# Layer 0 of a graph kernel, edge by edge: gathered rows of x times W1, float32r one-hot stacks, and W2 applied to sums per target node

## The chip, the core and the metric

The kernel runs on one core of a Trainium2 chip. The metric is the device time in microseconds (us) of one execution; the kernel before takes 5028.3 us, the median of three runs (5008.02 to 5033.12). The engines named below are TensorE (PE, with its weight loads as PEld), VectorE (DVE), ScalarE (ACT), GpSimd (POOL) and SyncE (SP), which only issues DMAs here. Each engine works through its own program in order and waits on semaphores.

## The reference

There are 12500 nodes with 48 features (x) and 200000 edges (src, dst), sorted by dst. Two layers follow each other, each with a residual and a layer norm:

```
layer 0:  h   = relu(concat(x[dst], x[src], e32) @ W1 + b1)      # 200000 x 128, W1 is 128 x 128
          msg = h @ W2 + b2                                      # W2 is 128 x 48
          x1  = layernorm(x + segment_sum(msg, dst))
layer 1:  m   = relu(x1[src] + e48)
          out = layernorm(x1 + (1 + eps) * x1 + segment_sum(m, dst))
```

The layer norm is over the 48 features, with no scale or offset. All arrays are float32.

## The kernel before

The edges are worked in 391 groups of 512 (4 tiles of 128 edges); 4 groups make an iteration of the loop. Since the edges are sorted by dst, the targets of one group lie within a window of 48 consecutive nodes. A prologue finds the window starts (base_row) and, for every edge, its place in the window (rel). If a group were wider than a window, a general path would be taken by a branch; with these inputs the windowed path runs.

Layer 0, for group u, as the engines do it:

- POOL gathers x[src] with four indirect DMAs, one for each tile, 128 rows of 48 floats each, into columns 48 to 96 of the tile edge (L427). It waits for S0["trans"] of four groups back, since there are four buffers.
- SP loads the 32 edge features into columns 96 to 128 of edge (L325), the indices (L315) and the 48 columns of xT that belong to the window, x_win (L349). SP works in the order of loads0: at the start of an iteration it also waits for the rows of the iteration before (next_idx).
- DVE writes the one-hot of the place in the window into columns 0 to 48 of edge, four instructions (L828).
- PE turns the four tiles by transposes into ps_t (L653), multiplies the window's rows by the first 48 rows of W1 (ps_a, L655), and ACT copies both to SBUF (edgeT, L526; w_edge, L534). One float32 matmul of 512 columns gives the hidden layer with features on partitions (ps_h, L662); ACT adds b1 and applies relu (hT, L538).
- One group later PE applies W2 to each tile (ps_m, L639), DVE adds b2 (msg, L848), PE sums the messages into the window by the one-hot (ps_sums, L629), and DVE adds the 48 x 48 result to the node sums acc (L844).

The order on each engine is written out by hand in one function for each engine (steps0). In the last 18 full iterations the layer norm of finished chunks of 1250 nodes is woven in (to_nodes L709, squares L503, sum_squares L940, divide L947, split L960 and L962, zero_sums L860); there are 10 chunks, the last of them after the loop. A float32 matmul is two passes of PE, and the trace has a record for each pass.

Layer 1 gathers rows of x1, but PE takes over three of every sixteen tiles by float32r matmuls of 480 columns against all of x1 (pick_rows, L699); these are what PE mostly does in layer 1. The change leaves layer 1's own steps as they are and gives them other PSUM banks.

## Time and profile before

| | |
|---|---|
| median of 3 runs | 5028.3 us |
| the profiled execution | 5031.79 us |
| its span (first to last instruction) | 5030.0 us |
| mean granted TensorE clock | 0.74 of full speed |
| PE busy | 4067.2 us, 81% of the span |
| DVE busy | 1776.9 us, 35% |
| ACT busy | 795.1 us, 16% |
| POOL busy | 2686.4 us, 53% |
| DMA | 149.71 MB, mean 30 GB/s |

The profiled execution's own time is 1.8 us more than its span and within the range of the three runs. The busy shares are means over two layers that have different limits: layer 0 ends at 2690.86 us (the last addition to acc before the last chunk's norm), and layer 1 takes the rest. Waits and prices have to be read by layer.

### The profile page before, as it was taken

The numbers are of one execution on the slowest core, as the hardware profiler recorded it, in microseconds if no ns is written. First come the engines' busy times: TensorE is split into PE (matmuls) and PEld (weight loads), VectorE is DVE, ScalarE is ACT, GpSimd is POOL, SyncE is SP. The second block draws the span as 40 slices with busy tenths as digits, with TensorE's granted clock in tenths as the row PEclk, the third lists the DMA queues.
The fourth block names the chain that finished last, engine by engine and source line by source line (L and its number), as shares of the span: only waits on it lengthen the run. The fifth ranks groups of instructions, "written<-read, shape, count | busy, mean of one in ns | idle before, by whom it ended". The sixth has DMA issues, their size and how long they took to land.

```text
span 5030.0 us, 74330 instructions
## 1 busy us (share of the span) xinstructions
PE 4067.2 (81%) x19093; PEld 2851.7 (57%) x19093; DVE 1776.9 (35%) x4614; ACT 795.1 (16%) x1962; POOL 2686.4 (53%) x2838
## 2 busy tenths in 40 slices
PE   5778887787887787888888777887887787878998
PEld 3455454454554454455556666665666665656777
DVE  2111111111111111122224455554555555545665
ACT  1222222222222222222221000000000000000111
POOL 5555555555555555555554555555454555554554
PEclk7666666656556656566567888889888888888988
DMA  3111111111111111111111111111111111111111
GB/s 66 27 25 26 27 26 26 27 25 25 26 27 25 26 27 26 25 28 29 28 31 29 29 31 32 29 31 32 29 29 29 33 29 29 32 31 29 37 38 35
DMA packets 409363, 149.71 MB, mean 30 GB/s; under 512 B 335252, under 2 KB 408936, under 8 KB 409192
## 3 DMA queue, kind: packets, MB, share of 16 engines
q0 software_dynamic: 90688, 69.83, 9.4%
q1 hardware_dynamic: 316392, 75.92, 7.5%
q10 hardware_dynamic: 2258, 3.68, 0.4%
q8 instruction: 10, 0.16, 0.0%
q14 instruction: 15, 0.12, 0.0%
HBM read 144.37 MB, written 4.80 MB: 30 GB/s over the span
## 4 chain that ended last, share of the span: by engine, by line
PE 63%; issue 15%; another core or an unknown queue 15%; DVE 4%; DVEq 1%; ACT 1%; DMA 0%; ACTq 0%; SPq 0%
PE ps_h L699 16%; PE ps_h L662 10%; PE ps_m L639 8%; PE ps_sums L629 8%; PE ps_t L699 8%; PE ps_t L653 6%; PE ps_a L655 3%; PE ps_nodes L709 1%; DVE at_place L881 1%; PE ps_t L691 1%; DVE picked L889 1%; PE ps_m L691 1%; DVEq L840 1%; ACT w_edge L534 1%
## 5 line engine op out<-in xcount | busy, mean ns | idle before, releaser
L427 POOL DMA_INDIRECT edge<-x,idx x1564 | 1482.5, 948 | 1191.4 <-issue 518.8
L427 POOL DMA_INDIRECT edge<-x_dram,idx x1270 | 1203.7, 948 | 1126.5 <-issue 611.1
L699 PE MATMUL ps_h<-x_parts,at_place 125*128 125x480 f32 x3920 | 1056.1, 422 | 83.3 <-issue 82.0
L629 PEld LDWEIGHTS ps_sums<-edge,msg 128*48 128x48 f32 x6256 | 452.1, 155 | 1105.0 <-issue 1096.9
L629 PE MATMUL ps_sums<-edge,msg 128*48 128x48 f32 x6256 | 567.7, 246 | 446.6 <-issue 274.6
L699 PEld LDWEIGHTS ps_h<-x_parts,at_place 125*128 125x128 f32 x3920 | 803.3, 211 | 220.9 <-issue 99.5
L662 PE MATMUL ps_h<-edgeT,w_edge 128*128 128x512 f32 x782 | 711.8, 1009 | 147.5 <-ACT w_edge L534 141.0
L844 DVE TENSOR_TENSOR acc<-acc,ps_sums 48x48 f32 x782 | 154.5, 198 | 1417.2 <-PE ps_sums L629 707.2
L699 PE MATMUL ps_t<-x_parts,at_place 125*128 125x480 f32 x1960 | 565.0, 425 | 100.7 <-issue 98.8
L639 PEld LDWEIGHTS ps_m<-w_sb,hT 128*128 128x128 f32 x3128 | 573.8, 275 | 127.3 <-issue 127.3
L639 PE MATMUL ps_m<-w_sb,hT 128*128 128x48 f32 x3128 | 630.5, 364 | 11.3 <-ACT hT L538 11.1
L848 DVE TENSOR_TENSOR msg<-ps_m,b_sb 128x192 f32<-128x192 f32 x391 | 139.7, 357 | 1158.6 <-remote 668.1
L699 PEld LDWEIGHTS ps_t<-x_parts,at_place 125*128 125x128 f32 x1960 | 406.7, 214 | 206.0 <-issue 150.0
L538 ACT ACTIVATE hT<-ps_h,b_sb 128x512 f32<-128x512 f32 x391 | 268.8, 687 | 1456.5 <-PE ps_h L662 670.5
L556 ACT ACTIVATE msg<-pre 128x192 f32<-128x192 f32 x391 | 141.7, 362 | 1842.3 <-DVE pre L909 915.8
L653 PE MATMUL ps_t<-ident_sb,edge 128*128 128x128 f32 x1564 | 388.6, 395 | 33.3 <-DMA x_win<-xT 23.4
L889 DVE SCALAR_TENSOR_TENSOR picked<-iota_sb,col_rest,ps_h 128x480 f32<-128x480 f32 x196 | 213.6, 1090 | 382.0 <-remote 183.7
L526 ACT ACTIVATE edgeT<-ps_t 128x512 f32<-128x512 f32 x391 | 233.1, 596 | 582.2 <-PE ps_t L653 268.9
L828 DVE TENSOR_SCALAR edge<-iota_sb,rel 128x48 f32<-128x48 f32 x1564 | 284.2, 254 | 60.3 <-issue 54.0
L653 PEld LDWEIGHTS ps_t<-ident_sb,edge 128*128 128x128 f32 x1564 | 252.2, 199 | 71.3 <-DMA x_win<-xT 23.5
L881 DVE TENSOR_TENSOR at_place<-ps_t,places_sb 125x1280 fp32r<-125x1280 f32 x197 | 291.7, 1481 | 0.0
L662 PEld LDWEIGHTS ps_h<-edgeT,w_edge 128*128 128x128 f32 x782 | 187.1, 294 | 159.5 <-ACT w_edge L534 153.0
(66 smaller groups left out, 1688.9 us busy)
## 6 DMA issues: line engine op xcount, KB each, us to landing
e_sb<-e SPq DMA_DIRECT2D x196, 192.0 KB
edge<-e SPq DMA_DIRECT2D x196, 128.0 KB
edge<-x,idx POOLq DMA_INDIRECT x1564
edge<-x_dram,idx POOLq DMA_INDIRECT x1270
idx<-src_tiles SPq DMA_DIRECT2D x392, 4.0 KB
x_win<-xT SPq DMA_DIRECT2D x391, 9.0 KB
acc<-xT ACTq DMA_DIRECT2D x1, 2343.8 KB, 24.4
x_dram<-feats SPq DMA_DIRECT2D x10, 234.4 KB
```

Source lines behind the costliest of these rows:

```text
L427: pool.indirect_dma_start(out=cols, out_offset=None, in_=rows_of, in_offset=bass.IndirectOffsetOnAxis(ap=index, axis=0)).then_inc(done, 16)
L526: nc.scalar.activation(edgeT[:, u % 2, :], ps_t[u % 2][:, :], ACT.Copy).then_inc(S0["edgeT"], 1)
L538: nc.scalar.activation(hT[:, u % 2, :], ps_h[u % 2][:, :], ACT.Relu, bias=b1_sb[:, :]).then_inc(S0["h"], 1)
L629: last = nc.tensor.matmul(sums, lhsT=msg[:, v % 2, t, :], rhs=edge[:, v, t, 0:WIN], start=(t == 0), stop=(t == TILES - 1))
L639: last = nc.tensor.matmul(ps_m[:, t, :], lhsT=hT[:, v % 2, t * P:(t + 1) * P], rhs=w2_sb[:, :], start=True, stop=True)
L653: last = nc.tensor.transpose(ps_t[u % 2][:, t * P:(t + 1) * P], edge[:, u, t, :], ident_sb[:, :])
L662: nc.tensor.matmul(ps_h[u % 2][:, :], lhsT=w_edge[:, u, :], rhs=edgeT[:, u % 2, :], start=True, stop=True).then_inc(S0["pre"], 1)
L699: last = nc.tensor.matmul(ps_picked[m], lhsT=at_place[:, m, c, :], rhs=x1_parts[:, c, part, :], start=(c == 0 and part == 0), stop=(c == C ...
L828: last = nc.vector.tensor_scalar(edge[:, (u + ahead) % UNROLL, t, 0:WIN], iota_sb[:, :], rel[:, bass.ds(i * UNROLL + u + ahead, 1), t], No ...
L844: nc.vector.tensor_tensor(acc[0:D, bass.ds(first, WIN)], acc[0:D, bass.ds(first, WIN)], ps_s[(u - back) % 2 if S is S1 else 0], ALU.add).t ...
L881: nc.vector.tensor_tensor(at_place[:, m, :, :], ps_place[m % 2].unsqueeze(1).to_broadcast([NP, CHUNKS, P]), places_sb[:, :].unsqueeze(2).t ...
L889: nc.vector.scalar_tensor_tensor(picked[:, :, :].rearrange("p f k -> p k f"), iota_sb[:, 0:CB].unsqueeze(2).to_broadcast([P, CB, D]), col_ ...
```

## The change

Layer 0 is built up anew; layer 1 and the general path keep their arithmetic.

- **A table.** Ahead of the loop PE multiplies all of x by the middle 48 rows of W1 (w1_src): 100 matmuls of 125 nodes by 128 features. ACT copies them out of PSUM (30 copies) and SP stores ten chunks of 640 KB to b_dram. Only then may the gathers of layer 0 start, and they fetch rows of 128 floats of this table, straight into the layout edge by feature. xT now comes in ten pieces on SP's queue.
- **Stacks.** A tile's stationary operand is now a stack (float32r, features on partitions, edges as columns): 48 rows of a one-hot of the window, computed directly in this layout by comparing dst ids, which SP loads broadcast to 48 partitions, twice (load_ids), and the edge features as a high and a low float32r part, turned by two transposes a group. Two tiles share a pair of 64-partition halves.
- **The moving operand** is w_edge, 256 columns: high and low parts of the window's product with W1 (with b1 as a 49th row) and of the edge features' weights. Four float32r matmuls a group write ps_h, edges on partitions; DVE adds both halves to the gathered rows (mix).
- **Relu and sums.** ACT and DVE write relu(h) as high and low parts beside a column of ones (h_parts); PE sums it over the edges into 48 x 258 by a one-hot (float32r). ACT copies the sums, PE turns them (turn_sums), and only then applies W2, once for 48 nodes instead of to 512 edges; b2 is added times the number of edges.
- The work is spread over slots with a lead of 1 or 2 groups (edge features) and lags of 1 to 4 groups (sums, turn, output, acc). The norm steps of two half chunks move to the second of two iterations.

```
-        x_win = sb("x_win", [D, UNROLL, WIN])
-        w_edge = sb("w_edge", [P, UNROLL, H])
-        edgeT = sb("edgeT", [P, 2, GE])
-        hT = sb("hT", [H, 2, GE])
+        x_win = sb("x_win", [SIDE, UNROLL, 2, SIDE])
+        w_edge = sb("w_edge", [P, 2, 2, 2 * H], F32R)
+        e_parts = sb("e_parts", [P, 2, TILES, 2 * DE], F32R)
+        sums_sb = sb("sums_sb", [WIN, 2, HS])
+        sumsT = sb("sumsT", [H, 2, WIN])
...
+            def load_ids(done, i, slot):
+                for p in (0, SIDE):
+                    sp.dma_start(dst_row[p:p + WIN, slot:slot + 2, :].rearrange("p g e -> p (g e)"),
+                                 dst_groups[bass.ds(i, 1), slot * GE:(slot + 2) * GE].to_broadcast([WIN, 2 * GE])).then_inc(done, 16)
...
-                        gather(edge[:, u, t, D:2 * D], rows_of, idx[:, u, t:t + 1], S["rows"][u])
+                        gather(edge[:, u, t, :] if S is S0 else edge[:, u, t, D:2 * D], rows_of, idx[:, u, t:t + 1], S["rows"][u])
...
-                others(S0, x, "trans")
+                wait_b_dram(pool)
+                gathers(S0, b_dram, "split", 0)
+                others(S0, b_dram, "split")
...
+            for n, c, first, end in thirds():
+                if first == 0:
+                    pe.wait_ge(s_xT[c], 16)
+                if n >= 4:
+                    pe.wait_ge(s_b_rows, n - 3)
+                for k in range(first, end):
+                    node = c * CN + k
+                    last = nc.tensor.matmul(ps_b[n % 4][0:NP, (k - first) * H:(k - first + 1) * H],
+                                            lhsT=acc[0:D, node:node + (NP - 1) * CB + 1:CB], rhs=w1_src[:, :], start=True, stop=True)
+                last.then_inc(s_b_nodes, 1)
...
+            def hidden(i, u):
+                b = u % 2
+                wait_group(pe, S0["mix"], i, u, back=1)
+                wait_group(pe, S0["alo"], i, u)
+                wait_group(pe, S0["spread"], i, u)
+                wait_group(pe, S0["edgeT"], i, u)
+                for t in range(TILES):
+                    j, side = divmod(t, 2)
+                    rows = P if side else SIDE + WIN
+                    last = nc.tensor.matmul(ps_h[:, t, :, :].rearrange("p a h -> p (a h)"), lhsT=stack[0:rows, b, j, side, :],
+                                            rhs=w_edge[0:rows, b, side, :], start=True, stop=True)
+                last.then_inc(S0["pre"], 1)
...
+            def sum_hidden(i, u, back):
+                for t in range(TILES):
+                    last = nc.tensor.matmul(ps_seg, lhsT=onehot_sb[:, b, t, :], rhs=h_parts[:, b, t, :],
+                                            start=(t == 0), stop=(t == TILES - 1))
...
+            def spread_ids(i, u, back):
+                for side in range(2):
+                    first = SIDE * (1 - side)
+                    ids = dst_row[first:first + WIN, v % UNROLL, :].rearrange("q (e j s) -> q s j e", j=2, s=2)
+                    last = nc.vector.tensor_scalar(stack[first:first + WIN, v % 2, :, side, :], ids[:, side, :, :],
+                                                   win_row[first:first + WIN, bass.ds(i * UNROLL + v, 1)], None, ALU.is_equal)
...
+            def mix(i, u):
+                wait_group(dve, S0["pre"], i, u)
+                dve.wait_ge(S0["rows"][u], i * (16 * TILES) + 16 * TILES)
+                nc.vector.tensor_tensor(edge[:, u, :, :], edge[:, u, :, :], ps_h[:, :, 0, :], ALU.add).then_inc(S0["first"], 1)
+                wait_group(dve, S0["first"], i, u)
+                nc.vector.tensor_tensor(edge[:, u, :, :], edge[:, u, :, :], ps_h[:, :, 1, :], ALU.add).then_inc(S0["mix"], 1)
...
+            def relu_low(i, u):
+                nc.vector.scalar_tensor_tensor(h_parts[:, b, :, H:2 * H], edge[:, u, :, :], 0.0, h_parts[:, b, :, 0:H].bitcast(F32),
+                                               ALU.max, ALU.subtract).then_inc(S0["split"], 1)
```

PE's program before, one group inside the loop of layer 0 (ps_t are the turned tiles, ps_m the messages):

```order
L653 MATMUL ps_t<-ident_sb,edge 128x128 [waits s0_rows1,s0_edgeT,s0_onehot]
L653 MATMUL ps_t<-ident_sb,edge 128x128 x3
L655 MATMUL ps_a<-w_dst,x_win 48x128
L639 MATMUL ps_m<-w_sb,hT 128x48 [waits s0_h,s0_msg]
L639 MATMUL ps_m<-w_sb,hT 128x48 x3
L662 MATMUL ps_h<-edgeT,w_edge 128x512 [waits s0_edgeT,s0_h,s0_stat]
L629 MATMUL ps_sums<-edge,msg 48x48 [waits s0_msg,s0_acc]
L629 MATMUL ps_sums<-edge,msg 48x48 x3
```

PE's program in the changed kernel at the same place (shared holds the stacks, the one-hots and h_parts; ps_eT the turned edge features):

```order
L798 MATMUL ps_h<-w_edge,shared 128x256 [waits s0_edgeT,s0_spread,s0_alo]
L798 MATMUL ps_h<-w_edge,shared 128x256 x3
L807 MATMUL ps_eT<-ident_sb,e_parts 128x128 [waits s0_elo]
L807 MATMUL ps_eT<-ident_sb,e_parts 128x128
L815 MATMUL ps_a<-w_dst,x_win 112x128 [waits s0_window1]
L825 MATMUL ps_hsum<-shared 48x258 [waits s0_split,s0_onehot,s0_sums]
L825 MATMUL ps_hsum<-shared 48x258 x3
L834 MATMUL ps_turned<-ident_sb,sums_sb 128x48 [waits s0_sums,s0_turned]
L834 MATMUL ps_turned<-ident_sb,sums_sb 128x48
L843 MATMUL ps_sums<-sumsT,w_sb 48x48 [waits s0_turned,s0_degree,s0_acc]
L844 MATMUL ps_sums<-ident_sb,b_deg 48x48
```

The hidden layer now stands first in a slot and works on group u; the transposes and the window's product belong to group u+1, the sums to u-1, the turn to u-2 and the output to u-3. The eight W2 matmul passes and the 512-column matmul are gone.

DVE's program before, one group inside the loop:

```order
L828 TENSOR_SCALAR edge<-iota_sb,rel 128x48 [waits s0_seg]
L828 TENSOR_SCALAR edge<-iota_sb,rel 128x48 x3
L848 TENSOR_TENSOR msg<-ps_m,b_sb 128x192 [waits s0_msgp,s0_seg]
L840 TENSOR_LOAD base_row
L840 ISA x2
L844 ISA [waits s0_seg,s0_acc]
L844 TENSOR_TENSOR acc<-acc,ps_sums 48x48
```

DVE's program in the changed kernel, one group inside the loop:

```order
L1063 TENSOR_TENSOR e_parts<-e_sb,e_parts 128x4x32 [waits s0_ehi]
...
L1074 TENSOR_SCALAR shared<-resid_sb,win_row 48x2x128
...
L1074 TENSOR_SCALAR shared<-resid_sb,win_row 48x2x128
L1082 TENSOR_TENSOR edge<-edge,ps_h 128x512 [waits s0_rows1,s0_pre]
L1084 TENSOR_TENSOR edge<-edge,ps_h 128x512 [waits s0_first]
...
L1091 TENSOR_SCALAR b_deg<-b_sb,sums_sb 48x48 [waits s0_sums,s0_out]
...
L1037 TENSOR_TENSOR acc<-acc,ps_sums 48x48
...
L1095 TENSOR_TENSOR shared<-iota_sb,rel 128x192
L1104 TENSOR_TENSOR w_edge<-ps_a,w_edge 48x128 [waits s0_ahi]
L1104 TENSOR_TENSOR w_edge<-ps_a,w_edge 48x128
L1111 SCALAR_TENSOR_TENSOR shared<-edge,shared 128x4x128 [waits s0_h]
```

DVE now has eleven arithmetic instructions a group where it had six, among them three over 512 columns. It, and no longer PE, waits for the gathered rows.

## Rows read from the trace of the kernel before

**Rows 1.** Busy time by stretch: start:end, length, each engine's us, PEclk, DMA share, GB/s.
```profile
10.00:20.00 10.00, 2.24 (x4) 1.01 (x4) 8.20 (x15) 1.49 (x2) 7.87 (x8) 1.00 1.33 214
...
500.00:1000.00 500.00, 400.90 (x1793) 250.10 (x1792) 93.92 (x449) 111.73 (x225) 280.60 (x297) 0.63 0.18 26
3500.00:4000.00 500.00, 393.78 (x1970) 303.07 (x1970) 257.54 (x441) 36.41 (x147) 255.04 (x269) 0.87 0.15 30
```

**Rows 2.** Instructions in order, one group of layer 0: start, us, engine, line [idle before].
```profile
1002.79 0.85 PE L629 MATMUL ps_sums<-edge,msg 128*48 128x48 f32 x8 [3.32 <-issue]
...
1003.76 1.11 PE L653 MATMUL ps_t<-ident_sb,edge 128*128 128x128 f32 x4
...
1004.80 0.66 PE L655 MATMUL ps_a<-w_dst,x_win 48*48 48x128 f32 x2
...
1005.39 1.94 PE L639 MATMUL ps_m<-w_sb,hT 128*128 128x48 f32 x8
...
1007.46 0.95 POOL L427 DMA_INDIRECT edge<-x,idx  x1 [2.71 <-remote]
...
1007.48 2.07 PE L662 MATMUL ps_h<-edgeT,w_edge 128*128 128x512 f32 x2
...
1008.71 0.95 POOL L427 DMA_INDIRECT edge<-x,idx  x1 [0.30 <-issue]
1009.48 0.15 PEld L629 LDWEIGHTS ps_sums<-edge,msg 128*48 128x48 f32 x1 [1.50 <-issue]
```

**Rows 3.** Groups of instructions, 500 to 1500 us: busy us, mean ns, idle before.
```profile
L427 POOL DMA_INDIRECT edge<-x,idx x589 | 557.4, 946 | 441.9 <-issue 190.9 <-PE ps_t L653 143.2 <-DMA idx<-src_tiles 71.3
```

**Rows 4.** PE's instructions in order, two stretches of layer 1.
```profile
3501.26 3.75 PE L699 MATMUL ps_h<-x_parts,at_place 125*128 125x480 f32 x16
...
3522.77 4.75 PE L699 MATMUL ps_t<-x_parts,at_place 125*128 125x480 f32 x11
```

**Rows 5.** Groups of DVE's and ACT's instructions over the whole span, shapes kept apart.
```profile
L889 DVE SCALAR_TENSOR_TENSOR picked<-iota_sb,col_rest,ps_h 128x480 f32<-128x480 f32 x196 | 213.6, 1090 | 382.0 <-remote 183.7 <-PE ps_h L699 125.9 <-PE ps_t L699 41.4
...
L844 DVE TENSOR_TENSOR acc<-acc,ps_sums 48x48 f32 x782 | 154.5, 198 | 1417.2 <-PE ps_sums L629 707.2 <-remote 548.1 <-issue 157.3
...
L909 DVE TENSOR_TENSOR pre<-edge,e_sb 128x192 f32<-128x192 f32 x391 | 136.4, 349 | 6.1 <-issue 5.7
...
L935 DVE SCALAR_TENSOR_TENSOR resid_sb<-feats,res_scale,ps_nodes 125x240 f32 x18 | 8.4, 464 | 53.5 <-remote 33.6 <-PE ps_nodes L709 17.2 <-issue 2.7
...
L526 ACT ACTIVATE edgeT<-ps_t 128x512 f32<-128x512 f32 x391 | 233.1, 596 | 582.2 <-PE ps_t L653 268.9 <-remote 191.2 <-issue 121.9
...
L534 ACT ACTIVATE w_edge<-ps_a 48x128 f32<-48x128 f32 x391 | 103.5, 265 | 27.2 <-PE ps_a L655 12.8 <-remote 5.9 <-issue 0.2
```

**Rows 6.** Gathers on POOL beside DVE's instructions, three places, in order of time.
```profile
17.27 0.51 DVE L819 TENSOR_SCALAR col_place<-resid_sb 128x392 f32<-128x392 uint32 x1
17.59 1.01 POOL L427 DMA_INDIRECT edge<-x,idx  x1 [0.30 <-issue]
...
18.82 0.85 DVE L822 TENSOR_TENSOR col_rest<-col_rest,resid_sb 128x392 f32<-128x392 f32 x1
18.91 1.59 POOL L427 DMA_INDIRECT edge<-x,idx  x1 [0.30 <-issue]
...
2452.57 0.95 POOL L427 DMA_INDIRECT edge<-x,idx  x1 [0.30 <-issue]
...
2453.42 0.41 DVE L962 TENSOR_TENSOR x_parts<-feats,x_parts  x1
```

**Rows 7.** First work of the loop, last sum of layer 0, and the last store of x1.
```profile
37.00 1.11 PE L653 MATMUL ps_t<-ident_sb,edge 128*128 128x128 f32 x4 [23.38 <-DMA x_win<-xT]
...
2690.86 0.20 DVE L844 TENSOR_TENSOR acc<-acc,ps_sums 48x48 f32 x1 [0.88 <-PE ps_sums L629]
...
2697.68 0.31 SPq L309 DMA_DIRECT2D x_dram<-feats  x1
...
2702.30 0.95 POOL L427 DMA_INDIRECT edge<-x_dram,idx  x1 [28.00 <-DMA x_dram<-feats]
```

More of the change, by code:

```diff
@@ L203, in build @@
         s_iota = sem("s_iota")
-        N_CONST = 16
+        N_CONST = 17
         def layer_sems(n):
-            per_slot = {"idx": 2, "edges": 2, "window": UNROLL, "rows": UNROLL}
-            counts = ("onehot", "awin", "stat", "trans", "edgeT", "pre", "h", "msgp", "sum", "msg", "seg", "acc",
-                      "parts", "zeroed", "column", "row", "places", "ten", "picked", "staged", "nodes",
-                      "resid", "square", "var", "std", "rstd", "norm")
+            per_slot = {"idx": 2, "edges": 2, "rows": UNROLL}
+            counts = ("onehot", "seg", "acc", "staged", "nodes", "square", "var", "std", "rstd", "norm")
+            if n == 0:
+                per_slot = {**per_slot, "window": UNROLL, "ids": 2}
+                counts += ("ehi", "elo", "trans", "edgeT", "spread", "awin", "ahi", "alo", "pre", "first", "mix", "h",
+                           "split", "sums", "degree", "turn", "turned", "out", "parts", "zeroed", "resid")
+            else:
+                counts += ("sum", "msg", "resid", "column", "row", "places", "ten", "picked")
             return {**{w: sems(f"s{n}_{w}", k) for w, k in per_slot.items()}, **{w: sem(f"s{n}_{w}") for w in counts}}
@@ L478, in general @@
             def general():
-                for u in range(UNROLL):
-                    pool.wait_ge(S0["rows"][u], 16 * TILES)
                 general_layer(G0, 0)
@@ new lines, in window_high, with relu_high @@
+            def window_high(i, u, back):
+                b = (u - back) % 2
+                wait_group(act, S0["pre"], i, u, back=back + 2)
+                wait_group(act, S0["awin"], i, u, back=back)
+                for side in range(2):
+                    first = SIDE * (1 - side)
+                    last = nc.scalar.activation(w_edge[first:first + WIN, b, side, 0:H], ps_a[first:first + WIN, :], ACT.Copy)
+                last.then_inc(S0["ahi"], 1)
+            def relu_high(i, u):
+                b = u % 2
+                wait_group(act, S0["seg"], i, u, back=2)
+                wait_group(act, S0["mix"], i, u)
+                nc.scalar.activation(h_parts[:, b, :, 0:H], edge[:, u, :, :], ACT.Relu).then_inc(S0["h"], 1)
@@ new lines, in copy_sums, with copy_turned @@
+            def copy_sums(i, u, back):
+                b = (u - back) % 2
+                wait_group(act, S0["turn"], i, u, back=back + 2)
+                wait_group(act, S0["degree"], i, u, back=back + 2)
+                wait_group(act, S0["seg"], i, u, back=back)
+                nc.scalar.activation(sums_sb[:, b, :], ps_seg, ACT.Copy).then_inc(S0["sums"], 1)
+            def copy_turned(i, u, back):
+                b = (u - back) % 2
+                wait_group(act, S0["out"], i, u, back=back + 2)
+                wait_group(act, S0["turn"], i, u, back=back)
+                nc.scalar.activation(sumsT[:, b, :], ps_sumsT, ACT.Copy).then_inc(S0["turned"], 1)
@@ new lines, in steps0 @@
+            def steps0(i, c):
+                for u in slots0(i):
+                    if exists(i, u, 0):
+                        hidden(i, u)
+                    if exists(i, u, -1):
+                        transpose_edges(i, u, -1)
+                        window_rows(i, u, -1)
+                    if exists(i, u, 1):
+                        sum_hidden(i, u, 1)
+                    if exists(i, u, 2):
+                        turn_sums(i, u, 2)
+                    if exists(i, u, 3):
+                        output_layer(i, u, 3)
+                    if c is not None and c[1] == 1 and u == 0:
```

415 lines of the change are left out of this document (283 added, 132 removed).

## The prediction

> **What bounds the kernel now.** I read the busy time by stretch first, since the page's shares are means over two layers. In [rows 1], layer 0 (500 to 1000 us) has PE busy 401 of 500 us at a granted clock of 0.63 and POOL busy 281; layer 1 (3500 to 4000 us) has PE at 394 us and 0.87. The clock has two levels, 1.2 and 2.4 GHz, so layer 0 runs mostly at the lower. Next the instructions in order, for one group of layer 0 [rows 2]: PE's five pieces take 0.85 + 1.11 + 0.66 + 1.94 + 2.07 = 6.63 us, and the next group's first piece begins at 1009.48, 6.69 us after 1002.79. So PE alone sets the pace at the lower clock; ACT's and DVE's pieces lie beside it. POOL's gathers follow each other at 1.25 us (1007.46 to 1008.71, 0.95 busy and 0.30 issue): four need 5.0 us and then wait [rows 2, 3]. Layer 0 ends at 2690.86 [rows 7], after 391 groups from about 37 us, or 6.79 us each. What remains to the end, 5030.0 - 2690.9 = 2339 us, is layer 1 and the last norm; 1.8 us lie outside the span.
>
> **PE's part.** Prices by the column, at the lower clock, since that one is the harder:
> - hidden, 4 float32r matmuls of 256 columns. Eleven of 480 columns took 4.75 us in a slow stretch, 0.90 ns a column, and sixteen took 3.75 us in a fast one, 0.49 [rows 4]. So 4 x 0.23 = 0.92 us (0.50 fast). The other bound is float32: 2.07 us for 512 columns [rows 2], or 4.1 us for the four. I take 0.92, as the rows have this very type.
> - two transposes, half of 1.11: 0.56. The window's product, two passes as before: 0.66.
> - sum_hidden, 4 of 258 columns: 0.93.
> - turn_sums, 4 passes of 128 x 48, half of L639's eight: 0.97. Output, 4 passes of 48 x 48, half of L629's: 0.43.
>
> Sum 4.47 us against 6.63. The eight W2 passes (1.94) and the 512-column matmul (2.07) go. PE falls below POOL's 5.0, even at 1.2 GHz, so no gain from the clock is counted.
>
> **DVE's part.** From 198 ns at 48 and 349 ns at 192 columns [rows 5]: 1.05 ns a column and 0.15 us each; L935 (464 ns for 240) adds 0.06 for a per-partition scalar. So edges_low (128) 0.28; spread_ids 2 x 256 columns 0.96; mix 2 x 512 columns 1.37; degrees 0.26; accumulate 0.20; onehot 0.35; window_low 2 x 128 columns 0.56; relu_low (512) 0.69. Sum 4.67 us, where DVE had 93.92 us in 500 [rows 1], 1.3 a group. The two spreads may run at two columns a cycle (about 4.4 in all). The high bound is the costliest instruction of the trace, L889, 1090 ns for 480 columns, 2.27 ns a column [rows 5]; with it for spread, mix and relu DVE needs 0.28 + 1.16 + 2.32 + 0.26 + 0.20 + 0.35 + 0.56 + 1.16 = 6.3. L889 writes every tenth word and the new ones write in order, like L935 and L909, so I take 4.67.
>
> **ACT's part.** 265 ns at 128, 596 ns at 512 [rows 5]: 0.86 ns a column. Turned edges 2 x 0.38, window 2 x 0.27, relu 0.60, sums (258) 0.38, turned 0.20, edges_high 0.27: 2.7 us, hidden.
>
> **The chain across engines.** hidden(u+1) waits for mix(u) and for window_low(u+1) on DVE, which waits for ACT's two copies, which wait for transposes and window product, which stand behind hidden(u) on PE: 0.92 + 0.56 + 0.66 + 0.54 + 0.56 and a few waits, about 3.5 us. The other half, mix 1.37 and then DVE's rest, is DVE's own 4.67. Neither reaches 5.0. SP loads the window of an iteration's first group only behind next_idx, that is, once the last group's rows are in; a store and its landing took 4.6 us here [rows 7], and a window a few. With POOL as the bound these rows arrive late and PE waits there, once in four groups; the four buffers let POOL go on meanwhile, so I add nothing and keep it for the range.
>
> **POOL is the new bound.** Same four gathers, 5.0 us a group, if a gather of 512-byte rows costs POOL what one of 192 bytes does. The trace has no other row length; POOL's 0.95 us are for 128 rows either way, and I take no change. DMA engines: a group moves 262 KB of rows, 197 KB of ids, 64 KB of features and some 20 KB more, 540 KB in 5.3 us or 102 GB/s, against 214 GB/s reached at 10 to 20 us [rows 1]. Covered, though it makes landings later.
>
> **POOL held by DVE.** In [rows 6] a gather that starts at 18.91 in the middle of L822, which has two SBUF inputs and ends at 19.67, takes 1.59 instead of 0.95 us: it gains 0.64, the 0.76 that were left less 0.12. One that starts in L819 with 0.19 left gains 0.06. The one at 2452.57, in progress when L962 (two SBUF inputs) starts, gains nothing. So a gather pays only where it starts inside such an instruction. The new slot has edges_low, onehot and relu_low of that kind, and perhaps the spreads. For a gather at a random moment the gain is the sum of (d - 0.12)^2 over twice the period: (0.03 + 0.05 + 0.32 + 0.26)/10.6 = 0.06 us, 0.25 for four. Bounds 0 and, with each instruction met at its start, 1.7. I take 0.3, so 5.3 us a group.
>
> The Trainium skill (SBUF — State Buffer, "SBUF: two separate sides") calls the shared port pair an exclusive lock, held for the whole instruction, in which the other side fully blocks, and warns that a VectorE instruction in a two-port mode keeps GpSimd from writing descriptors. [...]
>
> **The prologue.** The table is 100 matmuls of two passes over 128 columns. By L653's 0.28 us a pass [rows 2] this is 56 us at 1.2 GHz, about 30 if fast; ACT's 30 copies of at most 0.6 hide in it. xT arrives in pieces. The last of ten stores follows: 640 KB each. At 214 GB/s one takes 3.0 us and hides behind PE's 5.6 a chunk; by x1's last store (4.6 us from issue to the next gather for 234 KB [rows 7]) it would be 12.6. Start 8 + 56 + a store of about 9 gives the first gather at 73, I take 75; bounds 45 (fast PE) and 140 (stores in series). Before, the loop began at 37.
>
> **The sum.** 75 + 391 x 5.3 (2072) + 10 for the last rows to land and the lagging stages to empty + 15 for the woven-in norm steps (eleven instructions a chunk of about L962's 0.41 us [rows 6], 4.5 us of DVE for each of nine chunks, 40 in all; the slack of 0.6 us in each of 8 groups, 4.8 a chunk, would hide it if it were spread evenly, and I take a third as lost) = 2172, against 2691. Then 2339 as before, whose steps stay, and 1.8: **4513 us**. The profiled execution (5031.8) stands 3.5 above the median, within its runs, so I leave it at that and say 4513.
>
> **Rivals.**
> 1. *The slot doesn't close at POOL's rate.* DVE's 4.67 plus waits at each handover (mix after hidden, window_low after ACT, relu_low after relu_high), and late windows, give 5.9 us. For: DVE is 88% full and crosses to PE and ACT three times a slot. Against: PE before kept 6.69 with 6.63 of work. Time: 4513 + 0.6 x 391 = 4748.
> 2. *Clean gathers,* phases such that none starts inside a two-input instruction, and a faster prologue: 5.0 us and 50: 4370.
> 3. *Slower: DVE at L889's price.* 6.3 us of work and 0.5 of waits, 6.8 a group: 75 + 2659 + 25 + 2341 = 5100. It decides from 6.64 us a group on, where 391 groups eat the whole saving. Against it speak L909 and L935.
> 4. *Slower: the port is held at any overlap.* Then a gather waits for all of 0.28 + 0.35 + 0.69 + 0.96 us in turn, 7.3 a group: 5290. The row at 2452.57 speaks against it [rows 6]. [...]
> 5. *Gathers cost by the byte.* 0.95 x 512/192 = 2.5 us, 11.3 a group: 6860. Only the number of rows, 128 in all gathers, is seen to be constant, so it isn't excluded.
>
> **How the numbers follow.** Forecast 0.62 (its own range 4400 to 4640, from 5.0 to 5.6 us a group), rival 1 0.24, rival 2 0.06, rival 3 0.03, rival 4 0.02, rival 5 0.02, and 0.01 for no effect that can be told. The range for 8 in 10 is 4390 to 4780: 5.0 to 5.95 us a group. A measurement of this kernel can tell about 0.5% from no change (the runs of before lie within 0.5%). Faster: 0.62 + 0.24 + 0.06 = 0.92; same 0.01; slower 0.07.
>
> **What would show it.** Right: POOL's gathers follow at 1.25 us with few gaps from about 75 to 2150 us and DVE's first mix instruction waits for the rows; a group at 5.3; layer 1 as long as before; gathers of 1.2 to 1.6 us that start inside L1063, L1095 or L1111; PE near 4.5 us a group at the low clock. Rival 1: POOL waits for S0["split"] (L1111), and DVE has no idle time or has it behind PE or ACT. Rival 3: L1082 or L1111 over 1.0 us. Rival 4: gathers longer wherever DVE reads two inputs. Rival 5: gathers over 1 us with DVE idle. It would be wrong at its root if float32r at 256 columns cost like float32, or if layer 1 lost time by its new banks.

## The result, and the profile after

The changed kernel takes 5288.3 us, the median of four runs (5259.19 to 5299.72), beside 5025.5 for the kernel before (5008.02 to 5033.12): a ratio of 1.052, 95% interval 1.047 to 1.057. It is 5.2% slower; the forecast was 4513 us. A second comparison in another job gave 5214.7 against 4925.0, 1.060 (1.056 to 1.064).

One plain fact must be told first, since no number below can be read without it. The kernel before itself took 4910 to 5033 us in some jobs and 3686 to 3737 us in others, close together within each job. It isn't the chip: the one with number 2 took 4910 to 4944 us in one job and 3691 to 3704 us in another half an hour later. I call these *held* and *free* jobs, for what the traces will show. The forecast, the two results above and the profiles of before and after are from held jobs. Every experiment is read against the kernel before in its own job.

Where the difference lies. Layer 0 ends where layer 1's first gather starts; in the profile after, three rows tell the stages (minimum, median and longest duration in ns, then first and last start):

```profile
L515 POOL DMA_INDIRECT edge<-b_dram,idx x1564: 941/947/1822, 79.3 to 2911.5; - x196
```
```profile
L1082 DVE TENSOR_TENSOR edge<-edge,ps_h x391: 662/686/690, 86.0 to 2926.5; 128x512 f32<-128x512 f32 x196
```
```profile
L515 POOL DMA_INDIRECT edge<-x_dram,idx x1270: 941/947/1179, 2946.7 to 5258.7; - x182
```

The loop starts at 79 instead of 37, 42 us later. Layer 1 starts at 2946.7 instead of 2702.3 [rows 7]. From there to the end it is 2338.5 us, against 5030.0 - 2702.3 = 2327.7 before, 11 us more. (In the second job it was 28 us less, 2277 against 2305, so that is no cost of the change.) So 244 of the 255 us are the prologue and layer 0.

The stages by windows (columns as in [rows 1], whose rows 500:1000 and 3500:4000 these two answer):

```profile
500.00:1000.00 500.00, 348.33 (x1385) 257.24 (x1384) 294.43 (x756) 168.00 (x548) 266.54 (x278) 1.00 0.32 75
3500.00:4000.00 500.00, 431.39 (x1985) 310.25 (x1984) 254.18 (x434) 35.60 (x144) 256.47 (x271) 0.71 0.16 30
```

From 500 to 1500 us 138 groups pass (L1082 has 138 instructions there), 7.25 us each; before, 297 gathers in 500 us are 74 groups, 6.74 us each. No engine is busy over 70% of layer 0, POOL 53%. The page's slices say the same over the whole run, layer 0 up to slice 22:

```profile
PE   5667766666767766767777888888888888888998
DVE  2566555555655655556666554555455455545666
POOL 2555555555555555555555454555545555555554
PEclk9999999999999999999999877667777677777777
```

**PE's clock in layer 0.** The 1.00 and the 9s must not be read as full speed. The trace of after has no clock record before 2950 us, while that of before begins at 47 us, and a stretch without a record prints as 1.00. PE's own instructions tell the level. A transpose of 128 x 128 in the kernel before, in a stretch with a granted clock of 0.97, in one with 0.50 (windows 992:999 and 1003:1010), and at the very start, where 30:45 prints 1.00 though records begin only at 47; then the same kind of transpose after, over all of layer 0:

```profile
L653 PE MATMUL ps_t<-ident_sb,edge x8: 272/273/335, 992.4 to 996.9; 128*128 128x128 f32 x8
L653 PE MATMUL ps_t<-ident_sb,edge x8: 421/421/476, 1003.8 to 1011.0; 128*128 128x128 f32 x8
L653 PE MATMUL ps_t<-ident_sb,edge x8: 417/421/472, 37.0 to 41.6; 128*128 128x128 f32 x8
```
```profile
L807 PE MATMUL ps_eT<-ident_sb,e_parts x782: 415/421/478, 79.8 to 2921.5; 128*128 128x128 f32 x196
```

So PE ran the whole of the changed layer 0 at the lower level, 1.2 GHz. The same holds for every run below that is made from the changed kernel: none has a clock record ahead of layer 1, and none of their 782 such transposes took under 414 ns. Wherever their windows print 1.00 in layer 0, the lower level is meant. The windows of the kernel before at 500:1000 do have records.

What the engines wait for in 500 to 1500 us (engine, line, released by: total us, times, longest):

```profile
ACT shared L621 <- remote: 423.4, 58, 8.0
POOL edge L515 <- issue: 313.5, 521, 5.2
DVE edge L1082 <- remote: 271.0, 66, 5.9
POOL edge L515 <- DVE shared L1111: 153.3, 32, 6.1
```

"Remote" is a release that the profile finds no source for on this core. The program runs on one core, so it is no other core of its own. The kernel before has the same, in the same stretch:

```profile
DVE msg L848 <- remote: 257.2, 53, 8.1
...
ACT hT L538 <- remote: 235.4, 37, 8.4
```

One such wait in the timeline after (start, duration, instruction, idle time before it and what ended it):

```profile
995.20 0.31 ACT L657 ACTIVATE e_parts<-e_sb 128x128 fp32r<-128x128 f32 x1
...
995.57 1.22 PE L798 MATMUL ps_h<-w_edge,shared 112*128 112x256 f32 x4
...
996.59 0.63 PE L807 MATMUL ps_eT<-ident_sb,e_parts 128*128 128x128 f32 x2
...
997.10 0.95 POOL L515 DMA_INDIRECT edge<-b_dram,idx  x1 [0.30 <-issue]
...
998.35 0.95 POOL L515 DMA_INDIRECT edge<-b_dram,idx  x1 [0.30 <-issue]
...
1000.85 0.95 POOL L515 DMA_INDIRECT edge<-b_dram,idx  x1 [0.30 <-issue]
1001.33 0.69 DVE L1082 TENSOR_TENSOR edge<-edge,ps_h 128x512 f32<-128x512 f32 x1 [4.42 <-remote]
...
1003.33 0.39 PE L843 MATMUL ps_sums<-sumsT,w_sb 128*48 128x48 f32 x2 [3.38 <-issue]
...
1003.49 0.77 ACT L621 ACTIVATE shared<-ps_eT 64x256 fp32r<-64x256 f32 x2 [7.98 <-remote]
```

L621 needs nothing but the transposes L807, recorded as done at 997.2, and L798. It starts at 1003.5, and DVE's L1082, which needs L798 and the rows, at 1001.3, just as a run of eight gathers (991.94 to 1001.80) ends. After that POOL idles 5 us, as its next gathers wait for DVE, and the next pair of groups begins: a group of 5.7 to 6.4 us and one of 8.3 to 9.1 by turns, from L1082 to L1082 between 985.87 and 1015.32. The waits above say that it goes on so.

The trace's own semaphore records say which signal is late. The semaphore that L621 waits for is raised by PE behind the transposes; it is recorded at 1003.47, 6.3 us after their recorded end, and ACT starts 0.02 us later. In 63 of the 138 groups from 500 to 1500 us L621 starts more than 2 us after that end, and in 53 of the 63 within 0.1 us of such a record. In acc_wait_2, a free run (experiment 4), all 190 records stand within 0.02 us of the end. So in a held job PE's signal of being done comes late, or PE is done later than its modelled end says; what delays it is open.

It isn't the loading of instructions. The page's queue table has 11 and 18 packets on the two instruction queues in the whole run:

```profile
q8 instruction: 11, 0.18, 0.0%
q14 instruction: 18, 0.15, 0.0%
```

The Trainium skill (Runtime: NRT & Kernel Launch, "Instruction fetch mechanics") warns that a taken branch outside the two loaded pages of 16 KiB forces a fetch; the trace's packets have that size (0.18 MB / 11), but 29 of them can't be a fetch in each of 97 iterations. The counts are alike in held and free runs (10 and 15 in before, and in before_paced, a free one), and so is the time that the data packets take: 9.4% of 5030.0 us for the gathers' 90688 packets in before, 12.4% of 3748.0 in before_paced, 473 and 465 us.

### The profile page after: what moved, and what is told of

Its sections match the earlier page's. It is cut to its first block, busy times and chain, and to the rows that moved or that the text cites. A ratio compares the mean times of both kernels' runs of the same rounds, so it can differ in the third digit from the quotient of the medians.

```text
span 5285.2 us, 79584 instructions
## 1 busy us (share of the span) xinstructions
PE 4104.4 (78%) x17729; PEld 3039.9 (58%) x17729; DVE 2969.7 (56%) x6582; ACT 1195.8 (23%) x3948; POOL 2719.0 (51%) x2838
## 3 DMA queue, kind: packets, MB, share of 16 engines
q0 software_dynamic: 90688, 133.89, 12.3%
## 4 chain that ended last, share of the span: by engine, by line
PE 45%; another core or an unknown queue 25%; issue 14%; DVE 10%; ACT 3%; DVEq 2%; ACTq 1%; DMA 0%; SPq 0%
PE ps_h L894 17%; PE ps_eT L894 8%; PE ps_h L798 4%; PE ps_sums L784 3%; PE ps_hsum L825 3%; PE ps_turned L834 3%; DVE w_edge L1104 2%; PE ps_a L815 2%; ACT w_edge L631 2%; PE ps_eT L807 1%; DVEq L1032 1%; DVE shared L1074 1%; PE ps_nodes L904 1%; DVE edge L1082 1%
## 5 line engine op out<-in xcount | busy, mean ns | idle before, releaser
L515 POOL DMA_INDIRECT edge<-b_dram,idx x1564 | 1516.3, 969 | 1395.8 <-issue 855.9
L894 PE MATMUL ps_h<-x_parts,shared 125*128 125x480 f32 x3920 | 1167.0, 456 | 80.0 <-issue 78.5
L894 PEld LDWEIGHTS ps_h<-x_parts,shared 125*128 125x128 f32 x3920 | 812.6, 214 | 297.7 <-issue 95.5
L1082 DVE TENSOR_TENSOR edge<-edge,ps_h 128x512 f32<-128x512 f32 x391 | 265.7, 679 | 777.3 <-remote 700.9
L621 ACT ACTIVATE shared<-ps_eT 64x256 fp32r<-64x256 f32 x782 | 295.8, 378 | 1598.0 <-remote 1096.4
L798 PE MATMUL ps_h<-w_edge,shared 112*128 112x256 f32 (+1 forms) x1564 | 474.7, 455 | 233.1 <-DVE w_edge L1104 197.7
L894 PE MATMUL ps_eT<-x_parts,shared 125*128 125x480 f32 x1960 | 597.1, 453 | 48.6 <-issue 47.8
L798 PEld LDWEIGHTS ps_h<-w_edge,shared 112*128 112x128 f32 (+1 forms) x1564 | 362.4, 320 | 279.2 <-issue 151.1
L894 PEld LDWEIGHTS ps_eT<-x_parts,shared 125*128 125x128 f32 x1960 | 409.2, 214 | 178.2 <-issue 81.7
L834 PEld LDWEIGHTS ps_turned<-ident_sb,sums_sb 48*128 48x128 f32 x1564 | 362.0, 319 | 139.8 <-issue 139.7
L825 PE MATMUL ps_hsum<-shared 128*48 128x258 f32 x1564 | 427.7, 426 | 0.5 <-DVE shared L1111 0.5
L834 PE MATMUL ps_turned<-ident_sb,sums_sb 48*128 48x48 f32 x1564 | 424.9, 419 | 0.0
L807 PE MATMUL ps_eT<-ident_sb,e_parts 128*128 128x128 f32 x782 | 247.8, 421 | 85.7 <-DVE e_parts L1063 57.0
```

The lines of the kernel that those rows point to most:

```text
L515: pool.indirect_dma_start(out=cols, out_offset=None, in_=rows_of, in_offset=bass.IndirectOffsetOnAxis(ap=index, axis=0)).then_inc(done, 16)
L621: last = nc.scalar.activation(stack[side * SIDE:(side + 1) * SIDE, b, :, side, :], ps_eT[side * SIDE:(side + 1) * SIDE, 0, :, :], ACT.Copy)
L798: last = nc.tensor.matmul(ps_h[:, t, :, :].rearrange("p a h -> p (a h)"), lhsT=stack[0:rows, b, j, side, :], rhs=w_edge[0:rows, b, side, : ...
L807: last = nc.tensor.transpose(ps_eT[:, 0, j, :], e_parts[:, b, 2 * j:2 * j + 2, :].rearrange("p t f -> p (t f)").bitcast(F32), ident_sb[:, :])
L825: last = nc.tensor.matmul(ps_seg, lhsT=onehot_sb[:, b, t, :], rhs=h_parts[:, b, t, :], start=(t == 0), stop=(t == TILES - 1))
L834: last = nc.tensor.matmul(ps_sumsT, lhsT=sums_sb[:, b, a * H:(a + 1) * H], rhs=ident_sb[0:WIN, 0:WIN], start=(a == 0), stop=(a == 1))
```

## The experiments

Each edit is to the changed kernel unless said. "Left out after the first iteration" means that old data are used. Runs whose time is given without an interval were made once. Per group times are from the window 500:1000, where 20 PE instructions make a group of the changed kernel.

**1. The target ids.** Two broadcast loads of 192 KB come once in two groups, as the long waits do. DVE's wait for them goes with them.

```
-  wait_group(sp, S0["spread"], ...); load_ids(S0["ids"][u // 2], i, u)
+  if first_iteration(i): load_ids(S0["ids"][u // 2], i, u)
```

> The changed kernel with the broadcast loads of target ids (two of 192 KB per two groups) left out of layer 0 after the first iteration; stale ids are compared instead, the number of instructions on DVE stays. In the changed kernel a group of layer 0 takes 7.25 us, and on every second group DVE's first mix instruction (L1082) waits 4.4 us and ACT's turned edges (L621) 8 us, while POOL runs eight gathers in a row. Theory A, that the gathers running in a row are what holds the other engines: no change, 7.2 to 7.3 us a group, total 5240 to 5300. Theory B, that the bursts of ids clog the queue that everything else passes: the stalls go, 5.3 to 5.7 us a group, total 4520 to 4700.

**2. No gathers.** A semaphore is counted in their place, for layer 0 after the first iteration.

> The changed kernel with no gathers in layer 0 after the first iteration; POOL only counts, and DVE adds to old rows. Everything else stays. PE, DVE and ACT have 5.5, 4.8 and 3.1 us of work a group. Theory A: the stalls on L1082 and L621 vanish, and a group takes PE's 5.0 us or less, total about 4400 or below. Theory B (ids) or D (the wait of the output layer for the previous group's accumulate): the stalls of every second group stay, 6.5 us a group or more, total above 4950.

**3. Short rows.** Rows of x (192 bytes) instead of the table's 512; the rest of edge is set to zero at the start.

> The changed kernel gathering 48 floats (rows of x) instead of 128 in layer 0: as many gathers, 192 bytes a row instead of 512; the rest of each row in SBUF stays zero. Theory C, that the longer rows cause the stalls: 5.3 to 5.7 us a group, total 4520 to 4700. Theory A (it is the gathers being issued, not their bytes): 7.0 to 7.3 us a group, total 5190 to 5300.

**4. The accumulate's wait.**

```
 def output_layer(i, u, back):
-    wait_group(pe, S0["acc"], i, u, back=back + 1)
+    wait_group(pe, S0["acc"], i, u, back=back + 2)
```

On DVE the accumulate waits, instead, for DVE's own accumulate of the group before.

> The changed kernel with the output layer on PE waiting for the accumulate two groups back, as layer 1 does, instead of one (the accumulates are ordered on DVE itself). PE is idle 3.4 us before L843 in every second group. Theory D, that this wait closes a ring PE - DVE - PE: L843's idle time goes and a group takes 6 us or less, total 4800 or below. Theory A: PE runs on a little further and then waits in hidden (L798) instead, the group stays at 7.0 to 7.3, total 5190 to 5300.

This job was a free one: before took 3737 us. The four took 3882.6, 3792.5, 3879.8 and 3893.3 us, one run each. None of the four traces has a single remote wait, so each of my theories was asked in a place where the waits don't exist. What it showed is what the changed kernel is without them. Gathers of acc_wait_2, and the window of it and of no_gathers:

```profile
1003.62 0.95 POOL L515 DMA_INDIRECT edge<-b_dram,idx  x1 [0.30 <-issue]
1004.87 0.94 POOL L515 DMA_INDIRECT edge<-b_dram,idx  x1 [0.30 <-issue]
...
1016.61 1.46 POOL L515 DMA_INDIRECT edge<-b_dram,idx  x1 [0.30 <-issue]
```
```profile
500.00:1000.00 500.00, 474.17 (x1907) 353.62 (x1906) 420.59 (x1050) 245.86 (x764) 383.89 (x382) 1.00 0.41 104
```
```profile
500.00:1000.00 500.00, 500.00 (x2018) 374.24 (x2017) 442.75 (x1109) 258.89 (x807) 0.00 (x0) 1.00 0.23 57
```

The gathers follow without a pause: 382 in 500 us, one in 1.31 us, 5.24 us a group, with some stretched to 1.2 to 1.5. Bytes, ids and the accumulate's wait move nothing (3880 to 3893). Without gathers PE is busy all of the time and takes 500 / 100.9 = 4.96 us a group, at the lower clock.

**5. The same in a held job, and the kernel before beside it.**

> The kernel before, unchanged, for its profile beside the others. The same kernel took 5025 us beside the changed kernel and 3737 us beside the first four experiments, with PE at a granted clock of 0.86 instead of 0.73. Two explanations: the clock alone makes the difference (then every instruction of the profile is as before, PE's are shorter, and the waits of 4 to 8 us put down to an unknown source while POOL runs eight gathers stay); or the waits themselves are a property of how the program was running there and are gone (then none over 2 us is seen in layer 0, and POOL's 5.0 us a group or less is the pace, 1960 us for layer 0).

> The changed kernel, unchanged, timed against the kernel before on the same chip. If the program runs as in the first four experiments (before at about 3737 us), the changed kernel should stand at 3880 to 3900, 4% slower, since leaving out ids, row bytes or the wait for the accumulate moved nothing there; if it runs as at first (before at about 5025), 5259 to 5300. In the first case PE is the bound of layer 0 at 5.0 us a group at full clock.

For before_no_gathers the kernel before has its layer-0 gathers replaced by a count, as in 2.

> The kernel before with layer 0's gathers left out after the first iteration. Theory A (gathers in a row hold the others, and POOL's 5.0 us a group bounds the kernel before): layer 0 falls to PE's own work. At full clock that is 6.63 us at the lower level divided by at most 2, 3.4 to 4.5 us a group, 1370 to 1800 us for layer 0 instead of about 1960. Rival: PE is the bound of the kernel before in layer 0 on this chip also, and nothing moves.

> As no_gathers: the changed kernel without layer 0's gathers after the first iteration, beside the kernel before's own profile. If the program runs as in the first four experiments, 3790 us again: PE alone, 4.85 us a group. If it runs as at first (before at 5025), theory A says that the stalls of L1082 and L621 vanish and layer 0 takes 5.0 us a group or less, total 4400; the rival, an instruction supply that is slow whatever POOL does, keeps 6.5 us a group or more.

Measured: before 4935.0, after 5214.7, before_no_gathers 3815.6, no_gathers_again 4404.4. The windows of before_no_gathers and no_gathers_again:

```profile
500.00:1000.00 500.00, 490.49 (x3478) 319.35 (x3478) 180.49 (x868) 208.11 (x435) 0.00 (x0) 1.00 0.15 22
```
```profile
500.00:1000.00 500.00, 500.00 (x2018) 374.49 (x2018) 442.75 (x1109) 258.66 (x806) 0.00 (x0) 1.00 0.22 57
```

Without gathers the remote waits are gone from layer 0 of both (one of 1.0 us is left). The kernel before takes 3.45 us a group (435 ACT instructions, three a group) where it took 6.5, and 1119 us less in all; the changed kernel 4.96 where it took 7.0 (1421 PE instructions in after_again), and 810 us less. Layer 1, which kept its gathers, kept its waits. So in a held job taking the gathers away, and nothing of PE's work, frees both kernels. The two figures are at different clocks: without gathers the kernel before has PE at the upper level (its transposes take 273 ns in the median), the changed one keeps it at the lower (421), though PE is busy for all of the 500 us. At the lower level the change does cut PE's work, from 6.63 to 4.96 us a group.

**6. How many, in a row, or their traffic.** two_gathers leaves out two of four. paced adds one wait:

```
 wait_group(pool, S[read], i, u, back=UNROLL)
+if S is S0: wait_group(pool, S0["mix"], i, u, back=2)
```

plain_rows puts one plain load of 512 rows on SP in place of four gathers; pool_memset a memset of 1024 columns for each gather; before_paced holds the gathers of the kernel before until the transposes two groups back.

> The changed kernel with two of the four gathers of a group in layer 0, as two_gathers, which was run where before takes 3710 us and there gave 3791 (PE busy all the time, 4.96 us a group). Beside a kernel before of about 4925 to 5030: if every gather costs the others the same, 6.0 us a group and 4810; if only runs of more than four in a row do, 5.0 to 5.3 and 4410 to 4540.

> The changed kernel with its gathers also held until the mix of the group two back, as paced, which was 8.8% slower than before where before takes 3710 us. Beside a kernel before of about 4925 to 5030: if long runs of gathers hold the others, 5.3 to 6.2 us a group and 4530 to 4880; if each gather costs the same, 7.0 to 7.6 us and 5180 to 5400.

> The changed kernel with the four gathers of a group in layer 0 (after the first iteration) replaced by one plain load on SP of 512 rows of 512 bytes, the first of the table: the same bytes and the same number of rows in flight, but nothing that POOL writes. If the rows' traffic holds the others, the group stays above 6.5 us and the total above 4900 beside a kernel before of about 4925; if it is POOL's issue of gathers, 5.0 to 5.3 us a group, total 4410 to 4540. Where before takes 3710: 3790 to 3890.

> The changed kernel with each gather of layer 0 (after the first iteration) replaced by a POOL memset of 128x1024 float32 that no one reads: POOL is busy and counts as before, but nothing is written for a DMA and no rows move. If POOL being busy in SBUF (a port it shares) held the others, the waits of 4 to 8 us before L1082 and L621 stay in some measure, 6 us a group or more. If it is the gathers' own issue and DMAs, a group takes 5.0 us as with none (total 4400 beside a kernel before of 4925), or the memsets' own length if four are longer.

> The kernel before where POOL may start a group's gathers in layer 0 only when the group two back is transposed, instead of four back. Runs of eight gathers are cut to four. If long runs hold the others: layer 0 falls from 6.6 us a group towards POOL's 5.0, total 4300 to 4800 beside a kernel before of 4925. If each gather costs the same: 4900 to 4950.

Held job (before 4951.1 and, its own profile again, 4922.3): two gathers 4380.6, paced_2 5121.4, plain_rows 4410.3. Windows of two_gathers_2 and plain_rows:

```profile
500.00:1000.00 500.00, 500.00 (x2018) 374.47 (x2018) 444.48 (x1109) 258.51 (x806) 199.05 (x202) 1.00 0.34 83
```
```profile
500.00:1000.00 500.00, 500.00 (x2018) 374.40 (x2016) 442.91 (x1110) 258.58 (x806) 0.00 (x0) 1.00 0.42 111
```

Two gathers a group cost nothing, so it isn't a price for each gather. The same bytes in as many rows, at 111 GB/s in all, cost nothing, so it isn't the amount of traffic: what holds the others comes with POOL's gathers. (plain_rows reads the same 512 rows of the table each time and through SP's queue. So the scattered addresses and the gathers' own queue are left out with POOL's issue, and are not told apart from it.) The windows can't tell prices below PE's 4.96 us, which hides them. Pacing failed as a test of run length: in its trace runs of eight still occur (1009.44 to 1019.7), and up to 1020.9 to 1021.4 DVE's L1084 has stood idle for 4.3 us, ACT's L623 for 5.6 and PE's L817 for 4.4. Its 5121 us lie in neither expected range, 2% under the changed kernel of the second held job, which is too near to mean anything across jobs.

Free job (before 3709.5): two_gathers 3791.1, pool_memset 4228.6, paced 4039.8 (ratio 1.088, 1.081 to 1.095) and before_paced 3775.5 (1.019, 1.013 to 1.026; unclear by a bound of 2%). There pacing only delays: in paced SP's windows come late behind the rows that next_idx waits for (L817 waits 113 us in 1000 for x_win on PE, its weight load 131). pool_memset ran only here and so can't tell whether a busy POOL holds the others in a held job (experiment 7 bears on that); it shows another thing. Two DVE rows of it, and the same two instructions after:

```profile
L1090 DVE TENSOR_SCALAR shared<-resid_sb,win_row 48x256 fp32r<-48x256 int32 x327 | 369.2, 1129 | 7.7
...
L1101 DVE TENSOR_TENSOR edge<-edge,ps_h 128x512 f32<-128x512 f32 x164 | 112.5, 686 | 5.6
```
```profile
L1074 DVE TENSOR_SCALAR shared<-resid_sb,win_row 48x256 fp32r<-48x256 int32 x276 | 127.4, 462 | 6.5
L1084 DVE TENSOR_TENSOR edge<-edge,ps_h 128x512 f32<-128x512 f32 x138 | 94.8, 687 | 4.7
```

Beside POOL's memsets DVE's TENSOR_SCALAR takes 1129 ns instead of 462, and this TENSOR_TENSOR, with one input in SBUF and one in PSUM, is unchanged. So are those with both inputs in SBUF (L1079 276 ns for 282 after, L1112 370 for 359). The one exception is the accumulate of 48x48, 350 ns for 202, which isn't explained. Beside gathers neither of the two shown is longer: it is the gather that pays.

**7. At what rate.** Three gathers a group in layer 0, and in layer 1 a gap behind each gather:

```
 gather(...)
+if S is S1: nc.gpsimd.memset(busy_sb[:, :], 0.0)      # 128x512
```

> The changed kernel with three of the four gathers of a group in layer 0 (after the first iteration), and in layer 1 a POOL memset of 128x512 float32 that no one reads behind every gather. Beside a kernel before of about 4925 to 5030. Layer 0: three gathers take POOL 3.75 us of PE's 4.95 us a group. If the others are held whenever gathers come faster than one in about 1.8 us on average (7.2/4 here, 6.8/4 in the kernel before, 6.0/3.25 in layer 1), three give 5.4 us a group; if only POOL having no idle time holds them, 4.95 to 5.0; if each gather beyond two costs 1.1 us, 6.0. Layer 1: with the memsets a gather comes every 1.75 us at best, 5.7 us a group; if the gap relieves the others, layer 1 stays at 5.7 to 6.0 us a group (2230 to 2350 us); if the time that POOL spends is simply added, it rises to 6.5 or more. Where before takes 3710: layer 0 at 4.96 and layer 1 at 5.7 instead of 4.6.

Held job (before 5022.7): 4270.1 us, the fastest of all held runs. Its windows, and POOL in layer 1:

```profile
500.00:1000.00 500.00, 500.00 (x2017) 374.18 (x2017) 445.57 (x1108) 259.01 (x807) 308.64 (x304) 1.00 0.39 97
...
3000.00:3500.00 500.00, 417.22 (x2182) 333.39 (x2181) 294.11 (x482) 39.80 (x161) 445.59 (x598) 0.89 0.17 33
```
```profile
3504.88 0.95 POOL L520 DMA_INDIRECT edge<-x_dram,idx  x1 [0.17 <-POOL busy_sb L537]
3505.84 0.54 POOL L537 MEMSET busy_sb<- 128x512 f32 x1
3506.54 0.95 POOL L520 DMA_INDIRECT edge<-x_dram,idx  x1 [0.17 <-POOL busy_sb L537]
```

Three gathers in 4.96 us, one in 1.65 on average, cost nothing in this window either (a few remote waits, up to 7.3 us, stand elsewhere in layer 0). Within a group they still follow at 1.25 us, with a pause behind the third. And in layer 1, where POOL now has *more* to do and a gather follows in 1.66 us instead of 1.25, the remote waits are gone and the layer takes 4268.2 - 2123.7 = 2145 us instead of the 2266 to 2339 of the other held runs. That pace is POOL's own, 3.25 x 1.66 = 5.4 us a group, below both expected ranges; and POOL is busy there for 446 of 500 us, so a POOL that is busy with gathers and memsets in turn holds no one. So gathers hold the other engines, in a held job, when they go on at 1.25 us apart, and not when they come 1.66 us apart on average. Whether it is the mean rate, the pause, or POOL's wait between a gather and the next isn't told apart.

**8. The kernel before with gaps.**

> The kernel before, all of its work kept, with a POOL memset behind every gather: 128x256 float32 in layer 0, 128x384 in layer 1. By the 0.54 us of 512 columns and the 0.95 of 1024 these take about 0.33 and 0.43 us, and with the 0.95 of a gather and 0.17 between, a gather comes every 1.45 us in layer 0 (5.8 us a group) and every 1.55 in layer 1 (5.05). Beside a kernel before of about 4925 to 5030. If these gaps are enough: layer 0 falls from 6.7 to 5.8 us a group and layer 1 from 6.0 to 5.1, total 4150 to 4400, faster than both kernels by over 10%. If gathers must be 1.66 us or more apart: 4700 to 5000. If the time of POOL is simply added: 5100 and more. Where before takes 3710 us, no gathers hold anyone and POOL is the pace: 4200 to 4300, slower.

This job was a free one: 4338.1 us against 3699.4 (1.173, 1.170 to 1.175), slower as expected there (4200 to 4300). A gather came every 1.44 us in layer 0. Whether such a gap makes the kernel before faster in a held job wasn't run and stays open. No version beat both kernels with all of the work kept.

## Why the prediction was wrong, point by point

- **"So PE alone sets the pace at the lower clock": false, and the step that failed.** I took one group in which PE's instructions stood back to back [rows 2] for all of them, though its first row has 3.32 us of idle time before it. The window beside it said otherwise: 401 us busy in 500 over 74 groups is 5.4 us of PE a group, not 6.63 [rows 1]. A fifth of PE's time was idle, beside remote waits on DVE and ACT, and no term of the sum or rival stood for them. The change then cut PE's work at the lower clock from 6.63 to 4.96 us, and the group grew from 6.74 to 7.25: the saving was made on an engine that wasn't the pace. Without gathers the kernel before needs 3.45 us a group. For it the low clock was no fixed condition either: without gathers it read 1.00, by records, and its transposes took 273 ns. In the changed kernel the clock stayed low with gathers and without.
- **"PE falls below POOL's 5.0, even at 1.2 GHz": right, by a hair.** The sum was 4.47 us at the low clock and measured 4.96 there. Start to start in one group: hidden 1.02 for 0.92, transposes 0.56 for 0.56, window 0.69 for 0.66, sum 1.03 for 0.93, turn 1.01 for 0.97, output 0.65 for 0.43. My price by the column came from 480-column matmuls with a weight load each; here every 48 to 258 columns bring one, and those of the stacks are 0.23 us of busy time each (187.0 us for 808 in no_gathers_again). That this makes up the 0.49 us is likely, but no run shows it:

```profile
L805 PE MATMUL ps_h<-w_edge,shared 112*128 112x256 f32 (+1 forms) x808 | 246.4, 456 | 0.0
...
L805 PEld LDWEIGHTS ps_h<-w_edge,shared 112*128 112x128 f32 (+1 forms) x808 | 187.0, 320 | 18.3
```

  "So no gain from the clock is counted" came out true for the new kernel and missed what the old one could gain: 6.63 us at the lower level, 3.45 at the upper. What keeps PE at the lower level in the changed layer 0, even when it is busy without a break, wasn't tested.
- **"POOL is the new bound", 5.3 us a group: right in free jobs, wrong in held ones.** acc_wait_2 shows 5.24, from gathers stretched by DVE (1007 ns on average where 946 is the clean one), 0.24 us a group where I took 0.3. But POOL's 5.0 is nearly the pace of the kernel before there too: its paced form passes 397 gathers in 500 us. So nothing is won, and the prologue, the stretch and the norm's steps are lost: near 3890 against 3737. In held jobs the engines don't follow at 1.25 us, whichever kernel; 7.25 against 6.74 us a group. The term 391 x 5.3 was 1.95 us a group too small, 762 of the 775 us by which 4513 misses 5288.
- **"The buffers let POOL go on, so I add nothing": false in held jobs.** POOL goes on for eight gathers, then waits 5 us for DVE (L1111). Rival 1's sign, POOL waiting for the split, appeared, but with DVE 59% busy, not full: its mechanism was not this one.
- **DVE and ACT: right.** mix 2 x 0.69 (predicted 1.37 together), spread 0.91 to 0.97 (0.96), window_low 0.59 (0.56), relu_low 0.68 (0.69), relu 0.63 (0.60). Rivals 3 and 5 are out: nothing costs L889's price, and 512-byte rows cost POOL 947 ns as 192-byte ones did.
- **The port (rival 4): out.** A gather is 969 ns on average in layer 0, where rival 4 needed over half a microsecond more. By the Trainium skill (SBUF — State Buffer, "SBUF: two separate sides") the lock goes to whichever side starts first, and DVE takes it only in a two-port mode, or with two SBUF inputs against a GpSimd instruction that reads SBUF. The traces agree: the gather at 2452.57, begun before DVE's instruction, isn't stretched, and beside memsets TENSOR_TENSOR of 128x512 stays at 686 ns. The stretched TENSOR_SCALAR would fit a two-port mode, which no trace names; the accumulate's 350 ns for 202 doesn't fit.
- **The prologue and layer 1: right.** First gather at 79.3 for 75; layer 1 2338.5 for 2339. The norm and the drain cost more than the 25 us taken: in no_gathers_again layer 1 starts at 2106, where 79 + 391 x 4.96 is 2018.

The arithmetic of the loss in the first result: 391 x (7.25 - 6.74) = 199, the prologue 42, layer 1 11, in sum 252 of 255 us. Why a held group is half a microsecond longer after the change than before wasn't isolated. Between two waits the kernel before passes groups at the upper clock (4.1 us from transposes to transposes, 992.42 to 996.52), which the changed one can't at 4.96 us of PE; that would do it, and is only argued.

Open: what it is in a held job that the gathers take from the others. For layer 0 of the changed kernel it is shown, by single runs with effects of 800 us, that it goes away without POOL's gathers and with fewer of them, and that the same number of bytes and rows by SP's queue doesn't bring it on. Instruction loading is out by the packet counts. The ids and the length of the rows were varied only in a free job, where the waits don't exist, so a held job may still depend on them. In the profile after it is PE's signals that are recorded late; why is not shown.

## What to carry to other kernels

Divide an engine's busy time in a window by the groups in it before believing a tidy stretch of the timeline: 5.4 busy of 6.7 us is not a bound, and waits with no named source must be explained ahead of any saving. Check a printed clock against the duration of a known instruction: 1.00 here stood for missing records. Test what bounds a kernel by taking the suspected resource away (here the gathers: 1119 us) before rebuilding another engine's work. Time the unchanged kernel in more than one job.

## What the runs showed of the hardware

- The same program takes 3.69 to 3.74 or 4.91 to 5.03 ms in different jobs, on one chip even, and the difference appears with gathers 1.25 us apart.
- More work on POOL, a 0.54 us memset behind each gather, made layer 1 at least 5% shorter in a held job.
- A 128x128 transpose takes 273 ns at the upper clock and 421 at the lower. PE, busy for 500 of 500 us with 20 instructions in 4.96 us, stayed at the lower for a whole layer, while the kernel before without gathers, 490 of 500 us busy, ran at the upper.
- At the lower clock a float32r matmul of 256 or 258 columns with own weights takes 0.26 us from start to start, the passes of the output layer 0.16.
- POOL's memsets stretch DVE's TENSOR_SCALAR of 48x256 from 0.46 to 1.13 us; its TENSOR_TENSOR of 128x512 stays at 0.69.
